# A state-space mixer on one core: the sum over states by accumulating transposes

## The reference

```
h   = h * exp(delta_t * A) + (delta_t * x_t) * B_t      # per channel d and state n
y_t = sum over n of h[:, n] * C_t[n]
y   = y + xc * D_param
y   = y * silu(z)
x   = x + y @ out_proj_w.T
```

## Time and profile before

| what | value |
|---|---|
| median of three runs | 5010.67 us |
| profiled execution | 5014.11 us, span 5012.4 us |
| mixer | from 0 to about 2450 us of the span |
| experts | from about 2480 us to the end |
| busy over the span | PE 91%, DVE 50%, ACT 36%, POOL 34% |

### The profile page before, as it was taken

How to read it: one execution, slowest core, us unless ns; L and a number is a source line. 1 busy time by engine, 2 the same in 40 slices (tenths; PEclk the granted TensorE clock), 3 DMA queues, 4 the chain that set the end, 5 groups by cost and what they waited for, 6 DMA issues and landing times.

```text
span 5012.4 us, 72320 instructions
## 1 busy us (share of the span) xinstructions
PE 4547.6 (91%) x25508; PEld 3622.2 (72%) x25508; DVE 2489.4 (50%) x3168; ACT 1802.5 (36%) x3684; POOL 1709.4 (34%) x1214
## 2 busy tenths in 40 slices
PE   6788888888888888887499999999999999999999
PEld 5666666666666666665387887888888888888877
DVE  3999999999999999999300000000000000000000
ACT  6667667666767666675100000000000000000000
POOL 3667676666767666675200000000000000000000
PEclk8999999999999999999799999999999999999999
DMA  3111222221122222111310303103030030120300
GB/s 143 68 65 51 76 89 89 85 78 55 52 88 89 85 80 81 52 55 55 115 31 13 105 13 99 19 13 102 16 100 15 15 100 15 42 73 15 102 13 15
DMA packets 132812, 308.52 MB, mean 62 GB/s; under 512 B 8596, under 2 KB 17428, under 8 KB 124308
## 3 DMA queue, kind: packets, MB, share of 16 engines
q1 hardware_dynamic: 116564, 269.55, 15.5%
q0 software_dynamic: 14768, 34.41, 3.6%
q10 hardware_dynamic: 1296, 2.37, 0.1%
HBM read 920.96 MB, written 45.95 MB: 193 GB/s over the span
## 4 chain that ended last, share of the span: by engine, by line
PE 50%; ACTq 0%; DMA 0%; issue 0%; POOL 0%; DVE 0%; ACT 0%; SPq 0%; POOLq 0%; DVEq 0%
PE pA L1240 17%; PE pB L1240 17%; PE pD L1249 16%; PE pX L1227 1%; DMA rows_d<-pad 0%; ACTq L1208 0%; ACTq L1209 0%; DMA xr<-rows_d 0%; POOL out L1113 0%; ACTq L1207 0%; POOL tnum L1101 0%; DVE ow L1334 0%; ACT xT L1211 0%; POOL pad L1094 0%; SPq L1130 0%
## 5 line engine op out<-in xcount | busy, mean ns | idle before, releaser
L393 POOL TENSOR_TENSOR hs<-hs,bc 128x1024 f32<-128x1024 f32 x512 | 1214.0, 2371 | 424.7 <-DVE hs L833 402.5
L708 PE MATMUL pY<-hs,ident 128*128 128x256 f32 x4096 | 1051.5, 407 | 296.9 <-POOL hs L393 296.1
L833 DVE TENSOR_TENSOR_SCAN hs<-dA,pU 128x1024 f32<-128x1024 f32 x512 | 1169.4, 2284 | 28.5 <-DVE pU L823 2.2
L708 PEld LDWEIGHTS pY<-hs,ident 128*128 128x128 f32 x4096 | 801.1, 201 | 520.0 <-POOL hs L393 398.6
L1240 PE MATMUL pA<-xT,w1s 128*128 128x128 f32 x7504 | 992.0, 275 | 0.7 <-ACT xT L1211 0.7
L1240 PE MATMUL pB<-xT,w3s 128*128 128x128 f32 x7504 | 991.8, 275 | 0.0
L1198 ACT ACTIVATE gate<-pA 128x512 f32<-128x512 f32 (+1 forms) x268 | 145.8, 544 | 2310.1 <-PE pB L1240 2310.1
L1240 PEld LDWEIGHTS pA<-xT,w1s 128*128 128x128 f32 x7504 | 919.2, 192 | 32.7 <-issue 31.6
L1113 POOL DMA_INDIRECT out<-ow,trow x67 | 104.6, 1561 | 2437.2 <-DVE ow L1334 2400.5
L455 ACT ACTIVATE dA<-delta,aneg 128x255 f32<-128x255 f32 x2048 | 849.2, 509 | 221.7 <-DVE hs L833 206.7
L1240 PEld LDWEIGHTS pB<-xT,w3s 128*128 128x128 f32 x7504 | 914.1, 192 | 0.0
(11 more groups left out here) (162 smaller groups left out, 2373.8 us busy)
## 6 DMA issues: line engine op xcount, KB each, us to landing
w1s<-in_w SPq DMA_DIRECT2D x204, 1024.0 KB
w3s<-in_w SPq DMA_DIRECT2D x204, 1024.0 KB
w2s<-in_w SPq DMA_DIRECT2D x204, 1024.0 KB
win<-in_w_in SPq DMA_DIRECT2D x64, 1024.0 KB, 5.2
bc<-bc_d SPq DMA_DIRECT2D x64, 1024.0 KB, 4.7
w1s<-in_w SPq DMA_DIRECT2D x68, 512.0 KB
w3s<-in_w SPq DMA_DIRECT2D x68, 512.0 KB
w2s<-in_w SPq DMA_DIRECT2D x68, 512.0 KB
```

The lines of the kernel that those rows point to most:

```text
L393: pool.tensor_tensor(hs[b][:, :, :], hs[b][:, :, :], bc[:, N + g * PN:N + (g + 1) * PN, :], ALU.mult)\
L708: m = pe.matmul(pY[c % 2][:, 0:T], ident[:, :], hs[k % NB][:, i, :], start=False, stop=g == UPC - 1 and h == PPU - 1 and i == PN - 1)
L833: dve.tensor_tensor_scan(hs[b][:, :, :].rearrange("p n t -> p (n t)"), dA[b][:, :, :].rearrange("p n t -> p (n t)"), pU[:, :, :].rearrange ...
```

## The change

- The sum over states is made by transposes that accumulate: the weighed piece is the stationary operand, the identity the moving one, and 128 tokens by 128 channels land in the first half of the bank, as token rows. For each state there are two transposes of 128 columns in place of one product of 256 columns.
- When a chunk is complete, ScalarE copies the half bank to ysum (copy_y). TensorE then writes xc * D_param into the free half of the same bank and transposes ysum back onto it (turn_y: one product of 256 columns, two accumulating transposes). VectorE's finish reads that half.
- On ScalarE copy_y of chunk c stands at the end of beside(2c + 2). On TensorE turn_y of chunk c stands in slot 2c + 3, between the slot's two sums. On VectorE finish of chunk c moves from place (2c + 2, 3) to (2c + 4, 0). For the last chunks these places lie in the next step.
- The first part of the output projection moves from slot 2 to slot 3.

```diff
-        OUT_SLOTS = (2, 4, 5, 6)
+        OUT_SLOTS = (3, 4, 5, 6)
...
+                def copy_y(n, c):
+                    ge(act, summed, PIECES * n + PPC * (c + 1))
+                    ge(act, y_turned, CH * n + c - 1)
+                    act.activation(ysum[c % 2][:, :], pY[c % 2][:, 0:T], ACT.Copy).then_inc(y_copied, 1)
...
                 def beside(u):
+                    rest(u)
+                    if u == 0 and back:
+                        copy_y(r, CH - 1)
+                    if scan and u % UPC == 0 and u > 0:
+                        copy_y(s, u // UPC - 1)
...
+                def turn_y(n, c, nodd):
+                    ge(pe, y_copied, CH * n + c + 1)
+                    yT = pY[c % 2][:, T:2 * T]
+                    pe.matmul(yT, skip[:, c, :], xc[nodd][:, c, :], start=True, stop=False)
+                    for t in range(TT):
+                        m = pe.matmul(yT[:, t * P:(t + 1) * P], ysum[c % 2][:, t * P:(t + 1) * P], ident[:, :],
+                                      start=False, stop=t == TT - 1, is_transpose=True)
+                    m.then_inc(y_turned, 1)
+                def sums(u, h):
+                    c, g = u // UPC, (u % UPC) * PPU + h
+                    k = PIECES * s + PPU * u + h
+                    if g == 0:
+                        ge(pe, gated, CH * s + c - 1)
+                    ge(pe, weighed, k + 1)
+                    for i in range(PN):
+                        for t in range(TT):
+                            m = pe.matmul(pY[c % 2][:, t * P:(t + 1) * P], hs[k % NB][:, i, t * P:(t + 1) * P], ident[:, :],
+                                          start=g == 0 and i == 0 and t == 0, stop=g == PPC - 1 and i == PN - 1 and t == TT - 1,
+                                          is_transpose=True)
+                    m.then_inc(summed, 1)
...
                 for u in range(SLOTS):
                     beside(u)
                     if scan:
+                        sums(u, 0)
+                    if u == 1 and back:
+                        turn_y(r, CH - 1, 1 - odd)
+                    if scan and u % UPC == 1 and u > 1:
+                        turn_y(s, u // UPC - 1, odd)
+                    if scan:
+                        sums(u, 1)
...
-                    ge(dve, summed, PIECES * n + PPC * (c + 1))
+                    ge(dve, y_turned, CH * n + c + 1)
...
-                    if scan and u % UPC == 0 and c >= 1 and g == 3:
-                        finish(s, c - 1, odd)
-                    if back and at == (0, 3):
+                    if scan and u % UPC == 0 and c >= 2 and g == 0:
+                        finish(s, c - 2, odd)
+                    if back and at == (0, 0):
+                        finish(r, CH - 2, fodd)
+                    if back and at == (2, 0):
                         finish(r, CH - 1, fodd)
```

More of the change, by code:

```diff
@@ L109, in mixer @@
         delta = sb("delta", [P, CH, T])
+        ysum = [sb(f"ysum{i}", [P, T]) for i in range(2)]
         bc = sb("bc", [P, 2 * N, T])
@@ L209, in mixer @@
         summed = sem("summed")
+        y_copied = sem("y_copied")
+        y_turned = sem("y_turned")
         gated = sem("gated")
@@ L461, in copy_z, with rest @@
                     act.activation(szn[:, 2 * pair:2 * pair + 2, :], pM[pair % 2][:, :, :], ACT.Copy).then_inc(z_copied, 1)
+                def copy_y(n, c):
+                    ge(act, summed, PIECES * n + PPC * (c + 1))
+                    ge(act, y_turned, CH * n + c - 1)
+                    act.activation(ysum[c % 2][:, :], pY[c % 2][:, 0:T], ACT.Copy).then_inc(y_copied, 1)
                 def beside(u):
+                    rest(u)
[3 more added lines that the diff above has]
+                        copy_y(s, u // UPC - 1)
+                def rest(u):
                     if u == 0 and scan:
@@ L840, in finish @@
                 def finish(n, c, nodd):
-                    ge(dve, summed, PIECES * n + PPC * (c + 1))
+                    ge(dve, y_turned, CH * n + c + 1)
                     ge(dve, z_ready, n + 1)
-                    dve.tensor_tensor(sz[nodd][:, c, :], pY[c % 2][:, 0:T], sz[nodd][:, c, :], ALU.mult).then_inc(gated, 1)
+                    dve.tensor_tensor(sz[nodd][:, c, :], pY[c % 2][:, T:2 * T], sz[nodd][:, c, :], ALU.mult).then_inc(gated, 1)
                 spread = lambda v: v[:, :].rearrange("p (t a) -> p t a", a=1).to_broadcast([P, TT, E])
```

## The result

The changed kernel takes 5140.91 us (median of 4 runs, 5132.19 to 5148.71) against 5010.74 of the kernel before: ratio 1.0261, 95% interval 1.0248 to 1.0274. The profiled execution took 5148.71 us, its span is 5147.0. The forecast was 5085 and slower; the time lies above the range.

What follows compares the result with a forecast made beforehand. VectorE was taken to bound the mixer, TensorE the experts. 42.6 + 22 + 9 + 5 - 9.9 + 4.5 + 0.7 = 74 us on 5014.1 gave 5088, 5085 at the median; own range 5062 to 5112, wider 5035 to 5135.

Steps and rivals of the forecast that it cites:

- Part 4: finish at (4, 0) waits for the turn behind slot 3's projections: 3.4 us even, 2.7 odd steps, 42.6 us.
- Part 5: finish's waits for the other turns: 22 us for slot 9, 9 for slot 13, 5 for slots 1, 5, 7, 11.
- 0 to 1 us to spare: Turns of slots 1, 5, 7 and 11 come barely in time: 5 us of waits together, bounds 0 and 40.
- slot 9: finish waits for this turn as the clock falls in two steps of three: 22 us, bounds 1 and 82.
- slot 13: finish waits for this turn 1.5 us (0.8 odd) every second step, with the clock low: 9 us.
- Part 2: ScalarE's 128 more copies, 49 us in all, are hidden in its free time: cost 0, at most 49 us.
- part 3: Turning back on TensorE, one product and two transposes until VectorE sees the end, takes 0.87 us.
- Part 6: Small terms: finish's new place costs VectorE 4.5 us, residual waits of 9.9 us go, the mixer's end adds 0.7.
- Full clock: Rival: TensorE at full clock wherever it matters, only the waits at (4, 0) remain, 40 us, 5051; chance 0.25.
- Rival 3: TensorE's clock stays low in most of the mixer, transposes not counting as work: some 200 us, 5200; chance 0.09.
- Rival 2: Accumulating transposes cost as much as products, 1.8 us per piece, so finish waits longer: 5130; chance 0.06.
- Rival 4: Not slower: TensorE reaches the first turn in time, starting slot 3's projections while piece 5 is weighed: 5006; chance 0.15.

Runs made afterwards that it cites:

- products_p2_out2: The kernel before with finish at place (2c + 4, 2); sums stay products, no copy, no turn, output projection in slot 2: 4998.01 us, ratio 0.9978.
- places_only: The kernel before with only finish moved to (2c + 4, 0) and the output projection's first part to slot 3: 5000.4 us, ratio 0.9981.
- copy_twice: The changed kernel with each ScalarE copy made twice, the first to an unread tile: 5137.75 us, ratio 1.0261 to the kernel before.

## Why the prediction was wrong, point by point

- **The bound and the mechanism held.** VectorE sets the mixer's pace, TensorE's relief is worth the residual's waits (23.8 us in all fell to 13.9, the 9.9 of the earlier trace rows), and the wait at (4, 0) is a queue in TensorE.
- **Part 4 was mis-sized: 66.1 us in place of 42.6.** The step that failed is "TensorE is dense ahead of slot 3 and such stretches ran at full clock". That was read from the kernel before, where the output projection stands in slot 2 and the sums of pieces 4 and 5 follow it without a gap. The change takes this away itself: the projection leaves slot 2 and the sums are shorter, and TensorE is idle for 2.88 us ahead of piece 5. The clock falls to 0.50, and the sum and the projection behind the gap take 1.6 us longer than my count. With the idle time filled the count was right to 0.2 us.
- **Part 5 was mis-sized most: 40.8 us at (12, 0) and 22.0 at (2, 0), where I had 5 for four places.** I asked the clock question for slots 9 and 13 and not for the places that had "0 to 1 us to spare", where the same fall turns no wait into 4 us. My bound of 40 for these places was too low too: they have 72.6. The totals for slot 9 (22 against 22.6) and slot 13 (9 against 7.4) came out right partly by luck. For slot 9 I had 2.6 and 1.9 us in two steps of three; finish waited some 1.9 on even steps and 0.7 to 1.0 on odd ones, in every step but the last. For slot 13 I had 1.5 and 0.8 us in every second step; it waited 0.3 on most even steps and about 0.7 on most odd ones. I had too few waits, each too long.
- **Part 2 held** (a second copy costs nothing), **part 3 held**: in the rows above finish starts 0.85 us after the turn does (1363.01 to 1363.86), against 0.87.
- **Part 6 left out a gain.** I had 4.5 us more for VectorE. Up to the last residual addition its busy time fell from 2244.6 to 2219.9 us, mainly in three short instructions (below). With it the account closes: the mixer is 133 us longer, VectorE is idle for 158 more (finish 165 more, the residual 10 less, the rest 3) and busy for 25 less. The gain hid a part of my error in the waits, 165 us against 79.
- **Rivals.** Full clock (5051) is what the kernel with filled idle time shows: 5029, lower by part of the short instructions. The rule of the Trainium skill, TensorE: Matmul & The Clock Gate, Part 4 (PE-mode transpose), that transposes don't count as work for the clock, does not hold here: 0.94 with transposes against 0.93 with products at the same busy time, and transposes alone, put into the gaps, brought 0.82 to 0.91. Rival 3 had the right direction, some of its size, and the wrong cause; a mean of 0.82 between the levels 1.00 and 0.50 is the low one for about a third of the time, not most of it. Rival 2 falls: a piece takes 0.9 us (its own terms also add up to 5123, not 5130). Rival 4 falls: slot 3's projections start only behind the sum of piece 5, and finish waits.

## What to carry to other kernels

Before giving an engine less to do, look for what stands right behind its waits: if the shorter work makes TensorE's idle gap longer, the clock can fall, and the products behind it may cost more than was saved. When a result is handed back through an in-order queue, count all that is issued between the hand-over and the consumer, on both sides, and at both clocks; the four places that had 0 to 1 us to spare in my full-clock count waited 72.6 us. Take the state of an engine ahead of a place from the schedule after the change, not from the rows before it. The cheapest repair is distance: here one scan and one input term more between the turn and its reader took away 144 us.

## What the runs showed of the hardware

Some of VectorE's short instructions end when GpSimd's long one ends. The sum of two masks, sel, takes 0.15 us alone. In the kernel before, odd step:

```profile
1529.28 2.35 POOL L393 TENSOR_TENSOR hs<-hs,bc 128x1024 f32<-128x1024 f32 x1 [1.64 <-DVE hs L833]
1529.43 2.23 DVE L884 TENSOR_TENSOR sel<-oh 128x16 f32<-128x16 f32 x1
```

It starts 0.15 us after GpSimd's multiplication and ends with it, at 1531.66 and 1531.63. In the changed kernel there is no finish ahead of it at that place, and in the same step it is issued 0.16 us before GpSimd starts:

```profile
1615.42 0.15 DVE L917 TENSOR_TENSOR sel<-oh 128x16 f32<-128x16 f32 x1
1615.58 2.38 POOL L396 TENSOR_TENSOR hs<-hs,bc 128x1024 f32<-128x1024 f32 x1 [1.63 <-DVE hs L866]
```

Before, this is so in all eight odd steps; the other eight sel take 0.17 us. The 16 fell from 19.1 to 2.4 us, in all kernels with moved places. Two other forms get longer beside GpSimd's instruction: layer norm's ve (one of 1.01 us ends at 1373.50, GpSimd's at 1373.47) and rows (up to 1.59 us in place of 0.54). They fell from 54.4 to 28.5 in the changed kernel, but are as before in `products_p2_out2`. There sel's 16.7 us are more than the gain of 10.6; finish's own records are 2.7 us longer. In `places_only` VectorE is busy for 20 us less, and the residual waits 7 us more (30.9 against 23.8). The Trainium skill, SBUF — State Buffer, section Who interferes with whom, says that a VectorE instruction with two SBUF inputs contends with a GpSimd instruction that reads SBUF, and that the order of issue decides which of the two is blocked. The rows of sel, which has two, agree: 2.23 us behind GpSimd, 0.15 ahead of it.

The time of the changed kernel scatters by 16 us over 4 runs, that of the kernel before by 1.5 over 4 and by 8 over 23 others. In the profiled run finish waits 3.8 us at (12, 0) in two odd steps and 0.8 in most others; with `copy_twice` only one of them has 3.7. In all of these steps TensorE is idle for 2.4 to 2.7 us ahead of piece 21. So nearly the same idle gap does or doesn't bring the clock down from one step to the next. What decides it was not tried.
